# Experts of a convolution/attention/MoE kernel: fp32 products replaced by three products of rounded and remainder operands, part of the work per tile moved to GpSimd

## What is computed

```python
x = h.reshape(T, D)                      # layer-normed tokens, T = 12544, D = 256
probs = jax.nn.softmax(x @ gate_w + gate_b, axis=-1)      # E = 8
idx = jnp.argmax(probs, axis=-1)
pos = ...                                # place of the token in its expert, C = 1960 places
buf = jnp.zeros((E, C, D)).at[idx, pos_safe].set(x, mode='drop')
hmid = jax.nn.relu(jnp.einsum('ecd,edf->ecf', buf, w1) + b1[:, None, :])      # F = 1024
ybuf = jnp.einsum('ecf,efd->ecd', hmid, w2) + b2[:, None, :]
y_tok = ybuf[idx, pos_g] * (prb * kept)[:, None]
y = jnp.nan_to_num(y, nan=0.0, posinf=10000.0, neginf=-10000.0)
# and t = t + y
```

## Time and profile before

| | |
|---|---|
| median of 3 runs | 10340.24 us (10335.65 to 10344.37) |
| span of the profiled execution | 10375.5 us |
| PE busy | 8825.9 us (85%) |
| DVE busy | 5783.3 us (56%) |
| ACT busy | 4145.5 us (40%) |
| POOL busy | 3261.0 us (31%) |
| mean granted clock of PE | 0.81 of full |
| the experts | from about 9181 us to the end |

### The profile page before, as it was taken

One profiled execution on the slowest core, in us unless ns is written; L12 is line 12 of the kernel. 1 busy time (PEld: TensorE's weight loads), 2 busy tenths in 40 slices (PEclk: granted clock), 3 DMA queues, 4 the chain that ended last, 5 costly groups with the idle time before them and its releaser, 6 DMA issues. The chain is left out here.

```text
span 10375.5 us, 158377 instructions
## 1 busy us (share of the span) xinstructions
PE 8825.9 (85%) x47072; PEld 4663.3 (45%) x47072; DVE 5783.3 (56%) x13683; ACT 4145.5 (40%) x9073; POOL 3261.0 (31%) x1854
## 2 busy tenths in 40 slices
PE   4499989997667999998999989999999885448888
PEld 3355545554444444444444444444444334325555
DVE  4355555555557976675766757766676004324444
ACT  1255555553000055555555555555555660001111
POOL 2000000000000055555555555555555670142211
PEclk8655555555876599999999999999999996569999
DMA  4511121101533001202112021111211004211110
GB/s 137 88 20 20 20 35 20 20 8 49 178 123 103 10 20 28 56 21 56 27 24 56 19 56 30 31 45 30 47 28 41 14 5 127 78 40 42 44 34 21
DMA packets 368839, 480.22 MB, mean 46 GB/s; under 512 B 154040, under 2 KB 322362, under 8 KB 354855
## 3 DMA queue, kind: packets, MB, share of 16 engines
q1 hardware_dynamic: 344551, 426.24, 17.0%
q0 software_dynamic: 23424, 43.45, 1.6%
HBM read 298.80 MB, written 180.34 MB: 46 GB/s over the span
## 5 line engine op out<-in xcount | busy, mean ns | idle before, releaser
L1057 POOL TENSOR_TENSOR a_added<-a_P 128x896 f32<-128x896 f32 x1344 | 2805.3, 2107 | 3517.1 <-ACT a_P L1029 3516.8
L935 DVE TENSOR_REDUCE a_tops<-a_ps 128x1 f32<-128x448 f32 x5600 | 3166.2, 632 | 1322.8 <-PE a_ps L843 1319.5
L1029 ACT ACTIVATE a_P<-a_ps 128x448 f32<-128x448 f32 (+1 forms) x5600 | 2610.3, 548 | 2600.3 <-PE a_ps L901 2599.3
L901 PE MATMUL a_ps<-a_qp,a_kp 98*128 98x448 f32 (+1 forms) x5600 | 1946.8, 399 | 171.4 <-DMA a_qp<-scratch_neg 97.9
L843 PE MATMUL a_ps<-a_hk,a_hq 96*128 96x448 f32 (+1 forms) x4900 | 1922.6, 406 | 118.9 <-DMA a_hk<-scratch_k 96.8
L843 PEld LDWEIGHTS a_ps<-a_hk,a_hq 96*128 96x128 f32 (+1 forms) x4900 | 917.7, 188 | 1205.3 <-DVE a_tops L935 1047.2
L901 PEld LDWEIGHTS a_ps<-a_qp,a_kp 98*128 98x128 f32 (+1 forms) x5600 | 1008.0, 189 | 951.7 <-ACT a_P L1029 637.8
L860 PE MATMUL a_ps<-a_P,a_vt 128*32 128x448 f32 (+1 forms) x11200 | 1362.2, 558 | 0.0
L459 DVE CUSTOM_DVE_ANT_0 n_sm<-n_ps,n_bias 112x448 f32<-112x448 f32 x928 | 578.1, 624 | 850.8 <-PE n_ps L390 850.8
L485 ACT ACTIVATE n_P<-n_sm,n_mx 112x448 f32<-112x448 f32 x928 | 620.2, 668 | 845.4 <-DVE n_mx L459 845.4
L400 PE MATMUL n_ps<-n_idn,n_P 112*112 112x112 f32 x3712 | 923.5, 404 | 21.5 <-DVE n_P L466 21.5
(11 more groups left out here) (174 smaller groups left out, 6476.7 us busy)
## 6 DMA issues: line engine op xcount, KB each, us to landing
a_qp<-scratch_q SPq DMA_DIRECT2D x168, 224.0 KB, 3.8
a_hq<-scratch_q SPq DMA_DIRECT2D x84, 392.0 KB, 7.3
a_hk<-scratch_k SPq DMA_DIRECT2D x84, 392.0 KB, 8.6
a_kp<-scratch_k SPq DMA_DIRECT2D x96, 320.0 KB, 4.9
scratch_t<-o_ts SPq DMA_DIRECT2D x8, 3136.0 KB, 13.2
e_w<-in_w SPq DMA_DIRECT2D x16, 1024.0 KB
p_xs<-in_x SPq DMA_DIRECT2D x4, 3136.0 KB, 15.3
scratch_v<-p_vs SPq DMA_DIRECT2D x4, 3136.0 KB, 12.5
```

What stands on the lines that cost most here:

```text
L901: pe.matmul(PS[0:rows_of(t), i_s % 3, 0:GW], kp[0:98, hh, 128 * t:128 * t + rows_of(t)], qp[0:98, hh, GW * j:GW * j + GW], start=True, sto ...
L935: dve.tensor_reduce(tops[0:rows_of(t), KT * hh + t, k:k + 1], PS[0:rows_of(t), MAX + i % MAXES, 0:GW], AX_X, ALU.max).then_inc(topped, 1)
L1029: act.activation(P[0:rows_of(t), (2 * n + pair) % (2 * RING), hh % 2, :], PS[0:rows_of(t), (4 * n + hh) % 3, 0:GW], ACT.Exp).then_inc(expe ...
L1057: pool.tensor_tensor(added2[:, a % 6, :, :], P[:, (2 * n + pair) % (2 * RING), :, :], P[:, (2 * n + 2 + pair) % (2 * RING), :, :], ALU.add ...
```

## The change

Only `experts` changes.

- **Operands.** Each fp32 operand of the two stages becomes a rounded fp32r part (`w1h`, `w2h`, `xTh`, `hTh`) and an fp32r remainder (`w1l`, `w2l`, `xTl`, `hTl`). A product becomes three: high x high, low x high, high x low. PE thus issues six products a block in the hidden stage and 24 a tile in the output stage. Hidden blocks use four PSUM banks (`HID`, RH = 4) instead of three.
- **Weights.** w1 and w2 have one raw buffer instead of two and their own semaphore. POOL splits a slice of 256 columns per tile of the expert before (`split_weights`: cast, wait, subtract), 16 slices in all. PE starts an expert's hidden stage when all 16 are split. SP loads the raw weights when the ones before them have been split.
- **Tokens and hidden values.** ACT's copy now writes `xTh`; DVE subtracts it from PSUM (`low_of_turned`). ACT does relu twice, into `h32` (a ring of four) and `hTh`; DVE subtracts them (`low_of_hidden`), and ACT's block n waits for DVE's block n - 4.
- **Order.** DVE normalises group g+1 first, then does the subtractions of group g, then the tiles of group g itself: `scale(t)`, and `finish(t-1)` after it. The next expert's first group is normalised and turned within the last group of this one.
- **Tiles.** DVE's add and multiply are one `tensor_tensor_reduce`. `fin` and the clamp are done by POOL, which then scatters the tile before, gathers one tile, and splits a slice.

```diff
+            def split_weights(e, p, u):
+                if u == 0:
+                    pool.wait_ge(weights_loaded, (e + 1) * 32)
+                    pool.sem_inc(steps, 1)
+                if u < 8:
+                    c, at = u // 4, slice(256 * (u % 4), 256 * (u % 4) + 256)
+                    raw, high, low = w1[:, c, at], w1h[:, p, c, at], w1l[:, p, c, at]
+                else:
+                    raw, high, low = w2[:, u - 8, :], w2h[:, p, u - 8, :], w2l[:, p, u - 8, :]
+                pool.tensor_copy(high, raw).then_inc(high_made, 1)
+                pool.wait_ge(high_made, e * ST + u + 1)
+                pool.tensor_tensor(low, raw, high.bitcast(F32), ALU.subtract).then_inc(weights_split, 1)
...
             def expert(i, p, more):
                 e = 2 * i + p
-                if more:
-                    gather(e + 1, 1 - p)
                 for t in range(ST):
...
+                    pool.wait_ge(scaled, e * ST + t + 3)
+                    if t >= 2:
+                        pool.wait_ge(scattered[t % 2], e * (8 * ST) + 16 * (t // 2))
+                    else:
+                        pool.wait_ge(emptied, e + 1)
                     pool.sem_inc(steps, 1)
+                    pool.tensor_scalar(fin[0:s, t % 2, :], y[0:s, t % 2, :], 0.0, 0.0, ALU.mult, ALU.is_equal)
+                    pool.tensor_scalar(yf[0:s, t % 2, :], y[0:s, t % 2, :], -1.0e4, 1.0e4, ALU.max, ALU.min)\
+                        .then_inc(clamped, 1)
+                    if t >= 1:
+                        scatter(e, p, t - 1)
+                    if t < 4:
+                        gather(e, p, ST - 4 + t)
+                    elif more:
+                        gather(e + 1, 1 - p, t - 4)
+                    if more:
+                        split_weights(e + 1, 1 - p, t)
+                scatter(e, p, ST - 1)
...
-                        for c in range(CC):
-                            last = pe.matmul(PS[:, 2 + n % 3, 0:width(g)], w1[:, p, c, 128 * f:128 * f + 128],
-                                             xT[:, g % 2, c, 0:width(g)], start=(c == 0), stop=(c == CC - 1))
+                        terms = [(a[:, p, c, at], b[:, g % 2, c, 0:width(g)])
+                                 for c in range(CC) for a, b in ((w1h, xTh), (w1l, xTh), (w1h, xTl))]
+                        for k, (a, b) in enumerate(terms):
+                            last = pe.matmul(PS[:, HID[n % RH], 0:width(g)], a, b, start=(k == 0), stop=(k == len(terms) - 1))
                         last.then_inc(hidden, 1)
...
                         for f in range(FB):
-                            last = pe.matmul(PS[0:size(t), 5 + t % 2, 0:C],
-                                             hT[:, f, 128 * (t % 4):128 * (t % 4) + size(t)], w2[:, p, f, :],
-                                             start=(f == 0), stop=(f == FB - 1))
+                            if t == tiles[0]:
+                                pe.wait_ge(split_made, e * (SG * FB) + g * FB + f + 1 + RH)
+                            for k, (a, b) in enumerate(((hTh, w2h), (hTh, w2l), (hTl, w2h))):
+                                last = pe.matmul(PS[0:size(t), 5 + t % 2, 0:C], a[:, f, at], b[:, p, f, :],
+                                                 start=(f == 0 and k == 0), stop=(f == FB - 1 and k == 2))
...
                     for f in range(FB):
                         n = g * FB + f
+                        act.wait_ge(split_made, e * (SG * FB) + n + 1)
                         act.wait_ge(hidden, e * (SG * FB) + n + 1)
-                        act.activation(hT[:, f, 0:width(g)], PS[:, 2 + n % 3, 0:width(g)], ACT.Relu,
-                                       bias=b1[:, p, f:f + 1]).then_inc(relued, 1)
...
+                        act.activation(h32[:, n % RH, 0:width(g)], PS[:, HID[n % RH], 0:width(g)], ACT.Relu,
+                                       bias=b1[:, p, f:f + 1])
+                        if f == 0:
+                            act.wait_ge(made, e * ST + 4 * g + 4)
+                        act.activation(hTh[:, f, 0:width(g)], PS[:, HID[n % RH], 0:width(g)], ACT.Relu,
+                                       bias=b1[:, p, f:f + 1]).then_inc(plain_made, 1)
...
                 for g in range(SG):
+                    if g < SG - 1:
+                        normalise(ch, e, p, g + 1)
+                    elif more:
+                        normalise(ch, e + 1, 1 - p, 0)
+                    for f in range(FB):
+                        low_of_hidden(e, g, f)
+                    if g < SG - 1:
+                        low_of_turned(e, g + 1)
+                    elif more:
+                        low_of_turned(e + 1, 0)
+                    if g == 0 and more:
+                        tell(i + p, 1 - p)
                     tiles = range(4 * g, min(4 * g + 4, ST))
                     for t in tiles:
+                        scale(t)
+                        if t > tiles[0]:
+                            finish(t - 1)
+                    finish(tiles[-1])
```

More of the change, by code:

```diff
@@ L1366, in experts @@
         steps = sem("steps")
-        CHAIN = 3 * SG + 4 * ST
+        LN_CHAIN = 3
+        CHAIN = LN_CHAIN * SG + 3 * ST
         def size(t):
@@ new lines, in expert @@
+                    if t >= 1:
[7 more added lines that the diff above has]
+                scatter(e, p, ST - 1)
+            for u in range(ST):
+                split_weights(0, 0, u)
+            for t in range(ST - 4):
+                gather(0, 0, t)
@@ L1521, in expert, with scale @@
             def expert(i, p, more):
                 e = 2 * i + p
-                ch = Count(dve, chain, e * CHAIN)
+                ch = Count(dve, chain, e * CHAIN + LN_CHAIN)
+                def scale(t):
+                    s = size(t)
+                    y_ = y[0:s, t % 2, :]
+                    dve.wait_ge(made, e * ST + t + 1 + 4)
+                    dve.sem_inc(steps, 1)
+                    dve.tensor_tensor_reduce(out=y_, in0=PS[0:s, 5 + t % 2, 0:C], in1=b2b[0:s, p, :],
+                                             scale=tab[0:s, p, t, 1:2], scalar=0.0, op0=ALU.add, op1=ALU.max,
+                                             accum_out=widest[0:s, :]).then_inc(scaled, 1)
+                    dve.wait_ge(scaled, e * ST + t + 3)
+                    ch.after(dve.tensor_tensor(nan[0:s, t % 2, :], y_, y_, ALU.not_equal))
@@ L1561, in expert @@
-                    for t in tiles:
-                        s = size(t)
-                        if g >= 1:
-                            dve.wait_ge(turned, e * (CC * SG) + g * CC)
-                        dve.tensor_scalar(xn[0:s, t % 4, :], xg[0:s, p, t, :], mv[0:s, t, 0:1], rstd[0:s, t:t + 1],
-                                          ALU.subtract, ALU.mult).then_inc(normed, 1)
-                    if g == 1 and more:
-                        tell(i + p, 1 - p)
-                    if g >= 1:
-                        for t in range(4 * g - 4, 4 * g):
-                            finish(t)
@@ L1572, in expert @@
-                for t in range(4 * SG - 4, ST):
-                    finish(t)
-                assert ch.n == CHAIN, ch.n
+                        scale(t)
+                        if t > tiles[0]:
+                            finish(t - 1)
+                    finish(tiles[-1])
+                assert ch.n == CHAIN - (0 if more else LN_CHAIN), ch.n
             tell(0, 0)
+            first = Count(dve, chain, 0)
+            normalise(first, 0, 0, 0)
+            low_of_turned(0, 0)
             for_experts(dve, expert)
```

173 lines of the change are left out of this document (108 added, 65 removed).

## The result

The changed kernel takes 10456.16 us (median of 3, 10451.17 to 10465.08), the kernel before 10340.24: ratio 1.0115, 95% interval 1.0097 to 1.0134. Forecast were 10194 us and, with 0.76, a faster kernel. The number is that of the rival with slow POOL operations, to the microsecond, and that is luck: only part of that rival is what happened, as the runs show.

A forecast was written before the change was run, and what follows sets the result against it. POOL, at P = 5.2 us a tile, was to bound the output stage, giving groups of 30.3 us. Seven experts -122, the last -28, start +4 sum to -146, from 10340.2 to 10194 us; range 10090 to 10380.

The forecast's parts named there:

- the rival with slow POOL operations: Experts' tiles: POOL's short operations cost a microsecond each, P = 8.0 us, total 10456 us; chance 0.13.
- The forecast's own sum for a group: Experts, scale to scale of a group: G = 14.7 + 3P = 30.3 us, against 36.4 before.
- 3P: Output stage: three more tiles at POOL's pace, P = 5.2 us a tile, lowest 4.2, highest 7.1.
- PE has by then done the next hidden stage, and ACT four blocks: Group's chain: PE, free from about 9 us, needs 11; DVE's subtractions and ACT's other four blocks then take 7.7 together.
- the price of fin and clamp: POOL's part of an output tile: fin and clamp taken at 0.42 us each within P.
- The bound of the one-input price: POOL's one-input operations of 256 elements: 0.33 to at most 0.60 us, the latter at the two-input rate.
- The last expert: Last expert, which splits no weights: P = 4.6, G = 28.5, 114 us against 141.6, so -28 us.
- The rival of slow short products: Output stage on PE: short fp32r products no faster than 0.207 us, tile 5.0 us, total 10250 us; chance 0.10.
- a wait of PE at the expert's end for the last split: End of an expert: hidden stage starts only after POOL's last slice, at 20.7 us not 9; 7 us more than G.
- The start: Before the first expert: weight loads, 16 slices on POOL and gathers put the start at 9217.4, and low parts 2; +4 us.
- The port lock: Tiles: rival that DVE operations with two SBUF inputs hold POOL up, P = 6.3 us, total 10302 us; chance 0.17.
- The clock: Experts: rival that PE's clock stays at half, 10555 us, chance 0.05; forecast itself priced a cold output tile at nothing.

The follow-up runs named there:

- the late slices: Changed kernel with POOL splitting the next expert's weight slices after tiles 3, 7 and 11 instead of one after every tile; 10377.97 us, ratio 0.998.
- the version with three edits: Changed kernel with ACT's root behind the first four relus, fin and clamp on DVE, weight slices after tiles 3, 7 and 11; 10097.92 us, ratio 0.9713.

## Why the prediction was wrong, point by point

Forecast and measured time are 262 us apart. Of these 192 lie in the seven periods, 39 in the last expert and 2 in the start. The other 29 are an offset: the profiled run of the kernel before was 35 us over its median, that of the change 7 over its own.

The forecast's own sum for a group, 30.3 us, against the group that starts at 9564.07 (36.8). The normalisation of 4.0 is parted where ACT's root starts, 2.1 us into it in the trace of before (9653.35 to 9655.45):

| term | forecast | measured |
|---|---|---|
| first tile scaled and clamped | 1.4 | 3.0 (clamp ends 9567.1) |
| three more tiles, 3P | 15.6 | 16.9 (to 9584.0) |
| finish of the last | 1.6 | 1.5 (to 9585.4) |
| up to ACT's root | 2.1 of the 4.0 | 2.6 (to 9588.0) |
| root to the next scale | 1.9 + 7.7 | 12.8 (to 9600.85) |

- **The first step that failed is "PE has by then done the next hidden stage, and ACT four blocks".** It took PE's and ACT's blocks as free of DVE. ACT's queue was not read in its order: the root stands ahead of the relus, and what it waits for is the end of the tiles. Nothing hidden was done early but four blocks of PE, and all eight relu pairs lie behind the root instead of four. This is 3.2 of the 6.5 us of this group; the run that moves the root gives 11 us an expert and 78 in all.
- **The second is the price of fin and clamp**, 0.42 each "as these sizes are nearest the memset and cast rows": 1.13 and 1.07 measured. It makes the clamp of the first tile 1.6 later. P is 5.95 on average for 5.2 (the clamps start 4.8 to 6.5 us apart; the first gap of this group, with no scatter in it, is 4.85). That is 2.9 us in this group and 3.8 in the mean one, some 15 of the 28 us by which an expert's period of 155.9 passes the forecast's 128. The bound of the one-input price was 0.60, too low: the rival with a microsecond had the right price for two of its four operations, and cast (0.42) and subtraction (0.74) were as forecast.
- **Neither step alone makes the whole loss.** With the root moved, three groups of an expert take 33 to 36 us, which is the forecast's 30.3 with POOL's 3.8, and an expert is level with before (a period of 145.1 for 145.9; 10378.22 us in all, still 0.4% slower by the medians, where the offset of 35 us comes in). With the root left and `fin` and clamp on DVE the kernel is 0.8% faster. The rest, 11 us an expert, is ACT's root. The rival's 10456 has its P at 8.0, which no tile shows.
- **The last expert** was to gain 28 us and lost 11, and here the sum itself failed. The 114 us are four groups from the first scale on; the 141.6 they were set against start at the first normalisation, 32.4 us before the first scale. From first scale to the end the kernel before takes 109.2, so that the forecast's own terms give +5 and not -28. That is 33 of the 39 us. The two causes above make the other 6: they work in its first two groups (32.9 and 34.8 us; the last two, with no next group to normalise, 25.7 and 26.6).
- **Right:** the products. fp32r products of 512 columns start 0.23 us apart and those of 256 columns 0.12 (the forecast had 0.213 to 0.237 and 0.107 to 0.118). PE's busy time fell from 124 to 101 us an expert, where 86 to 94 were forecast. Half clock is little of that, as it is still 98.7 with the clock at 1.00; counted by starts (192 x 0.23, 384 x 0.12, and 4 for the transposes) it is 94. The rival of slow short products falls. Right too: a wait of PE at the expert's end for the last split (102.7 us in six), +5 us for 7; DVE's waits for the clamp; POOL idle in the hidden stage. The forecast's own sign of being wrong, fin or clamp at 0.8 us or more, is what came.
- **The start**, +6 for 4, is right by luck: the first normalisation starts at 9227.0 where 9217.4 was forecast, and from there to the first scale it is 24.4 us, where it was 29.8.
- **The port lock** as priced (1.7 us a tile) is no large part of the change: cast and subtraction take 0.42 and 0.74 beside DVE, and 0.40 and 0.72 at the start of the experts, where DVE stands. It shows where DVE subtracts in a row, and the other way round at L68, where DVE waits 0.5 us a group for POOL; the forecast had no term for that.
- **The clock** fell to 0.80, not to 0.5. In 9589.5 to 9593.0 it was half, behind PE's pause, for the first eight products; they are on the chain, and the forecast priced that at nothing. ACT had four blocks in hand, so most of it is hidden: at ACT's own pace, 1.14 us a block, the eighth pair would have started at 9596.15, and it starts at 9597.00. So 0.85 us of this group is an estimate of what it costs at most; no run takes the clock by itself.

## What to carry to other kernels

When an operation is to be hidden "while the other engine waits", write down each engine's queue in order and look for the first instruction in it that waits for the slow part. One small root in front of eight independent relus made everything behind it serial. Before work goes to a slow engine on a path that goes tile by tile, measure the very instruction in the very shape: a cast of the same size is no measure for a `tensor_scalar`, and a pair of operations taken at 0.84 us that costs 2.2 is, on a path that passes it 16 times an expert, the largest term of the outcome. When a sum is set against a measured stretch, both must start at the same event. Small fixed work for later (a weight slice) belongs where the path does not run through that engine, and not beside work of another engine that it slows.

## What the runs showed of the hardware beyond what was expected

- POOL, 128 x 256 fp32: cast 0.42 us, subtraction 0.74, `tensor_scalar` with one operator 0.85 to 0.92, with two 1.07 to 1.13. The Trainium skill, "GPSIMD Engine Reference", section "Elementwise — side-by-side cycle accounting", gives 1.03 cycles an element for a body of at most two operations and 2.6 for two inputs, at 1.2 GHz; an estimate from it for 256 elements is 0.22 and 0.55 us, without the dispatch, for which it has a figure of DVE alone. Cast and subtraction (0.40 and 0.72 at the start of the experts, where DVE stands) agree with that if some 0.17 us of each is fixed. The `tensor_scalar`, with one input, costs far more (1.07 to 1.09 with DVE idle), and the section does not name it.
- POOL's subtraction beside seven DVE subtractions in a row took 3.66 us for 0.74.
- DVE's `tensor_scalar` is held up by POOL's subtraction: 0.65 to 0.69 us for 0.17 at 128 x 4 (26 of 26 times, ending with it), and 2.3 to 2.4 for 1.4 for four of 128 x 256 beside the late slices.
- fp32r products of 256 columns start 0.12 us apart at full clock, each with its own weight load of 128 columns.
- PE's granted clock in the experts followed its pauses: 0.80 with 11 us pauses in each group, 0.94 to 1.00 by expert in the version with three edits, 0.66 when two thirds of its products are left out.
